# A block-diagonal product in four array tiles of 64 rows by 64 columns, placed between the projections and the transposes, with the projections in the order V, Q, K

## The chip, the cores and the metric

The kernel runs on one core of one Trainium2 chip. The metric is the device time in microseconds of one execution. The kernel before takes 1122.14 us as the median of three runs, from 1119.28 to 1123.42 us.

## The reference, cut to what matters

One transformer block on x of 128 sequences with 32 tokens of 512 features (4096 rows), in fp32. Each sequence has a style id (0 to 15) and an adapter id.

```python
def cond(x, ids, W):                  # W: 16 matrices of 32 x 32
    return einsum('bct,bcd->bdt', x, W[ids])
h = cond(x, itok_B_0_15, cond_weights)
qkv = clip(einsum('bsd,ed->bse', h, w_qkv), -8, 8)
q, k, v = split(qkv); q, k = layer_norm(q), layer_norm(k)
scores = einsum('bqhd,bkhd->bhqk', q, k) * 0.25 + alibi   # 32 heads of 16, causal
x = x + einsum('bsd,ed->bse', softmax(scores) @ v, w_out)
y = einsum('bsi,boi->bso', x, adapter_weight[adapter_ids])
x = x + ffn(y)                        # relu squared, a routed low-rank part, layer norm
```

What matters here is the first line. For each sequence its 32 x 512 slab of x is multiplied, over its 32 token rows, by a 32 x 32 matrix. Tokens mix only inside a sequence.

## The kernel before, in words

**Tiles.** The 4096 rows are cut into 32 tiles of 128 rows, which are four sequences each. The vector engine sorts the sequences by adapter first, so that most tiles have one adapter. The first half of the program handles attention and the adapter product, tile by tile, in a loop over i from 0 to 30 and a tail written out by hand. The second half is the feed-forward part in 8 groups of 4 tiles; the change doesn't touch it.

**The order is written out by hand on every engine.** There is one program per engine, and each iteration of its loop i holds pieces of several tiles at once: the projections of tile i, the transposes of tile i-1, the scores of tile i-2, the softmax-weighted sum of tile i-3, the output projection of tile i-4 and, from i = 6 (`LAG`), the adapter product of tile i-6. Semaphores join the engines: `upto(e, name, t)` makes engine e wait until the step `name` of tile t is done.

**The style product.** GpSimd builds `style_bd`, 128 x 128, which holds the four 32 x 32 matrices of a tile on its diagonal and zeros elsewhere (L1726). TensorE multiplies by it in `style` (L691): four fp32 matmuls, one for each 128 features, with x as the stationary operand and `style_bd` as the moving one; the result, h transposed, fills bank 6. ScalarE rounds it to fp32r as `h_hi` (L1197), VectorE takes the rest as `h_lo` (L1510).

**The projections.** `project` (L701) makes 12 matmuls for each of Q, K and V: high by high, high by low and low by high, over four chunks of features. Q goes to bank 2, K to bank 3, V to bank 5. VectorE clips each out of its bank (`take_q`, `take_k`, `take_v`, L1419), with layer norm statistics for Q and K behind the clip (L1583, L1604).

**One iteration on TensorE, from i = 6.** Projections Q, K, V; `turn_slot` (L796), `turn_values` (L735) and the turns of Q and K (L761), which are transposes in two array tiles of 64 rows by 128 columns; `style` of tile i+1; `scores` (L778) in eight array tiles of 64 rows by 32 columns; `adapt_slot` (L814), 12 matmuls into bank 5; `out_project` (L750), 12 matmuls into bank 6; `values` (L718) in four array tiles of 128 rows by 32 columns. The turned Q and K lie side by side in banks 2 and 3, the turned slot and values in banks 4 and 7.

**The other engines in the same iteration.** VectorE: transpose of the probabilities (L1517), the division (L1465, L1469), clip and statistics of Q, `w_low` (L1424), or `y_low` in the last iterations, clip and statistics of K, clip of V, the low parts `xgT_lo` (L1433), `o_lo` (L1529), `h_lo` (L1510), bias and maximum (L1442, L1446), `q_lo` and the low part of K (L1454, L1460), the residual (L1479). ScalarE: `p_hi` (L1182), a weight chunk, `w_hi` (L1101), normalization of Q and K (L1264), then the high parts `xgT_hi` (L1093), `o_hi` (L1192), `v_hl` (L1256), `h_hi` (L1197), scaling of Q and K (L1227, L1234), their high parts (L1242, L1251), the adapter output `ys` (L1110), the exponential (L1177). GpSimd: two gathers, `w_lo` (L1774), small steps of the layer norm, `p_lo` (L1780), subtraction of the maximum (L1768), the low part of V, `style_bd`.

```python
                for c in range(KC):
                    m = e.matmul(B6[:, P * c:P * c + P], xt[t % XR][:, P * c:P * c + P],
                                 style_bd[t % 2][:, :, :].rearrange("p j d -> p (j d)"), start=True, stop=True)
```

Of the kernel before, what the change touches and what calls it, by code (L numbers as in the profile page):

```python
# [98 lines left out]
def program(nc, x, style_ids, adapter_ids, style_w, wqkv, wo, qk_ln, w2, w_up, w_down, fc1t, expert,  # L99
# [34 lines left out]
    B5, B6 = (psum(f"bank{i}", [P, DM])[:, :] for i in (5, 6))  # L134
# [263 lines left out]
    def values_halved(t):  # L398

        return slot_halved(t + 4 - LAG) and t + 4 >= LAG  # L400

# [16 lines left out]
    with nc.Block() as block:  # L418
# [264 lines left out]
        def _(e):  # L683
            def style(t):

                e.wait_ge(a_x[t % XR], 16 * (t // XR + 1))
                upto(e, "style", t)
                upto(e, "x1", t - 6)
                upto(e, "hlo", t - 1)
                for c in range(KC):  # L690
                    m = e.matmul(B6[:, P * c:P * c + P], xt[t % XR][:, P * c:P * c + P],  # L691
                                 style_bd[t % 2][:, :, :].rearrange("p j d -> p (j d)"), start=True, stop=True)
                m.then_inc(A["h"], 1)
# [108 lines left out]
            def adapt_slot(s, into):  # L802
# [3 lines left out]
                upto(e, "cv" if s < LAST else "cq", s + LAG)  # L806
                if s:
                    e.wait_ge(d_mc, s)
                pairs = [(xgT_hi, w2_lo, c) for c in range(KC)]
# [174 lines left out]
            for i in range(T - 1):  # L984
                if 0 < i < SHORT:
                    style(i + 1)
                project_q(i)
# [5 lines left out]
                project_v(i)  # L993
                if i >= LAG:
                    turn_slot(i - LAG, banks47)
# [7 lines left out]
                if i >= LAG:  # L1003
                    style(i + 1)
# [81 lines left out]
        def _(e):  # L1086
# [107 lines left out]
            def high_h(t):  # L1194
                upto(e, "h", t)
                upto(e, "pv", t - 2)
                e.activation(h_hi[t % 2][:, :, :], B6.rearrange("p (c t) -> p c t", c=KC), ACT.Copy) \  # L1197
# [69 lines left out]
            for i in range(T - 1):  # L1267
# [20 lines left out]
                if i >= LAG:  # L1288
                    slot_in(i - LAG, banks47)
# [3 lines left out]
                if i >= SHORT:  # L1293
                    high_h(i + 1)
# [122 lines left out]
        def _(e):  # L1417
# [89 lines left out]
            def low_h(t):  # L1507
                upto(e, "hhi", t)
                upto(e, "pv", t - 2)
                e.tensor_tensor(h_lo[t % 2][:, :, :], B6.rearrange("p (c t) -> p c t", c=KC),  # L1510
                                h_hi[t % 2][:, :, :].bitcast(F32), ALU.subtract).then_inc(A["hlo"], 1)
# [95 lines left out]
            for i in range(T - 1):  # L1607
                if i >= 3:
                    turn_probs(i - 3)
                if i >= 4:  # L1610
                    divide(i - 4)
                take_q(i)
# [10 lines left out]
                take_v(i)  # L1623
                if i == 0:
                    low_weights(3)
                if i >= LAG:
                    low_slot(i - LAG, banks47)
                if i >= 4:
                    low_o(i - 4)
                if i >= SHORT:  # L1630
# [286 lines left out]
```

## Time and profile before

| | |
|---|---|
| median of three runs | 1122.14 us (1119.28 to 1123.42) |
| profiled execution, its own time | 1117.33 us |
| its span | 1115.5 us |
| mean granted TensorE clock | 0.991 of full |
| TensorE busy | 1068.9 us, 96% |
| VectorE, ScalarE, GpSimd busy | 622.4, 570.1, 565.3 us |

A row of a timeline gives the start in microseconds from the span's start, the length, the engine (PE is TensorE's matmul, PEld its weight load, DVE VectorE, ACT ScalarE, POOL GpSimd), the line of the kernel, the operation, what it writes from what, the array tile for matmuls (rows*columns), the operand shape and how many instructions were merged into the row; in brackets stands idle time before it and who ended it. An fp32 matmul shows as two records, one fp32r or bf16 matmul as one. The length of a matmul record includes its way through the array, so the distance between starts tells the pace.

### The profile page before, as it was taken

Reading aid. Unit: us, or ns where it says so; the run is one execution under the profiler, and the core shown is the slowest. Engines: PE = TensorE matmul, PEld = TensorE weight load, DVE = VectorE, ACT = ScalarE, POOL = GpSimd, SP = SyncE. Lnnn points to the kernel's source line nnn. Section 1 sums busy time; section 2 is a strip of 40 time slices with the busy share of each in tenths; the row PEclk is TensorE's granted clock in tenths of the full one; section 3 lists DMA queues with packets and bytes.
Section 4 is the critical chain, followed back from the end, with each engine's and each line's share of the span. In section 5 each row is a group of like instructions: output and inputs, shape, how many; then the busy total and the mean of one; then the engine's idle time right before and its main releaser. Section 6 shows DMA issues by size and latency. Waiting matters only on the chain.

```text
span 1115.5 us, 28260 instructions
## 1 busy us (share of the span) xinstructions
PE 1068.9 (96%) x11412; PEld 848.4 (76%) x11412; DVE 622.4 (56%) x1050; ACT 570.1 (51%) x955; POOL 565.3 (51%) x490
## 2 busy tenths in 40 slices
PE   5999999999999999999989599999999999999994
PEld 3878888888887888888778476777878787787883
DVE  4677767676766677666765124444544534454432
ACT  3576777777777777777775203424060514232220
POOL 5666877777776767776745112323242323233331
PEclk9999999999999999999999899999999999999998
DMA  6225454555545455555477927443526253130101
GB/s 255 62 79 174 170 185 162 185 167 181 176 171 187 160 187 188 193 159 182 144 263 263 349 89 219 168 95 128 147 71 198 63 192 91 39 85 29 48 29 38
DMA packets 99984, 166.52 MB, mean 149 GB/s; under 512 B 45648, under 2 KB 46416, under 8 KB 96016
## 3 DMA queue, kind: packets, MB, share of 16 engines
q1 hardware_dynamic: 90304, 140.97, 38.5%
q0 software_dynamic: 6064, 17.05, 5.2%
q10 hardware_dynamic: 3488, 6.70, 1.8%
q8 instruction: 92, 1.51, 0.6%
q14 instruction: 36, 0.29, 0.1%
HBM read 98.09 MB, written 40.89 MB: 125 GB/s over the span
## 4 chain that ended last, share of the span: by engine, by line
PE 87%; DMA 3%; issue 3%; POOL 2%; DVE 2%; ACT 1%; SPq 1%; ACTq 0%; DVEq 0%; POOLq 0%
PE pair L934 15%; PE banks L910 15%; PE banks L701 14%; PE bank L750 7%; PE bank L701 7%; PE bank L814 7%; PE bank L927 4%; PE banks L927 4%; PE bank L691 3%; PE pair L718 3%; PE pair L778 2%; PE banks L830 2%; DMA xm<-x_rows 1%; PE banks L880 1%; PE banks L761 1%
## 5 line engine op out<-in xcount | busy, mean ns | idle before, releaser
L1774 POOL TENSOR_TENSOR w_lo<-w2t,w_hi 128x2048 fp32r<-128x2048 f32 x26 | 119.5, 4595 | 70.5 <-ACT w_hi L1101 70.5
L1839 POOL TENSOR_TENSOR u_lo<-act,u_hi 128x512 fp32r<-128x512 f32 x64 | 82.5, 1289 | 124.3 <-ACT u_hi L1313 124.3
L1863 POOL TENSOR_TENSOR frstd<-fve,cst 128x1 f32<-128x1 f32 x32 | 31.9, 996 | 195.9 <-DVE fve L1707 195.9
L1700 DVE TENSOR_TENSOR total<-total,pair 128x512 f32<-128x512 f32 x32 | 22.0, 688 | 168.5 <-PE pair L934 168.5
L701 PE MATMUL banks<-wqkv_hi,h_hi 128*128 128x512 f32 x256 | 103.4, 404 | 0.7 <-DVE wqkv_lo L1575 0.5
L910 PE MATMUL banks<-yT_hi,up_hi 128*128 128x512 f32 x256 | 101.4, 396 | 0.0
L1646 DVE TENSOR_TENSOR act<-act 128x512 f32<-128x512 f32 x59 | 63.0, 1068 | 66.8 <-ACT act L1309 66.8
L701 PE MATMUL banks<-wqkv_hi,h_lo 128*128 128x512 f32 x256 | 99.9, 390 | 0.0
L701 PE MATMUL banks<-wqkv_lo,h_hi 128*128 128x512 f32 x256 | 99.9, 390 | 0.0
L910 PE MATMUL banks<-yT_hi,up_lo 128*128 128x512 f32 x256 | 99.8, 390 | 0.0
L910 PE MATMUL banks<-yT_lo,up_hi 128*128 128x512 f32 x256 | 99.7, 389 | 0.0
L934 PE MATMUL pair<-down_hi,u_hi 128*128 128x512 f32 x256 | 99.6, 389 | 0.0
L934 PE MATMUL pair<-down_lo,u_hi 128*128 128x512 f32 x256 | 99.6, 389 | 0.0
L934 PE MATMUL pair<-down_hi,u_lo 128*128 128x512 f32 x256 | 99.6, 389 | 0.0
L1768 POOL TENSOR_TENSOR probs<-probs,row_max 128x1024 f32<-128x1024 f32 x32 | 61.4, 1918 | 52.4 <-DVE row_max L1446 52.3
L1309 ACT ACTIVATE act<-banks 128x512 f32<-128x512 f32 x64 | 37.9, 592 | 82.6 <-PE banks L910 82.6
L1780 POOL TENSOR_TENSOR p_lo<-probsT,p_hi 128x1024 bf16<-128x1024 f32 x32 | 68.9, 2155 | 9.4 <-ACT p_hi L1182 9.3
L1409 ACT ACTIVATE total<-banks,weight 128x512 f32<-128x512 f32 x16 | 11.0, 687 | 120.5 <-PE banks L927 120.5
L1313 ACT ACTIVATE u_hi<-act 128x512 fp32r<-128x512 f32 x64 | 40.1, 626 | 44.1 <-DVE act L1646 44.0
L910 PEld LDWEIGHTS banks<-yT_hi,up_hi 128*128 128x128 f32 x256 | 48.1, 188 | 13.9 <-issue 4.2
L701 PEld LDWEIGHTS banks<-wqkv_hi,h_hi 128*128 128x128 f32 x256 | 48.0, 188 | 13.2 <-issue 1.4
L701 PEld LDWEIGHTS banks<-wqkv_hi,h_lo 128*128 128x128 f32 x256 | 48.0, 188 | 10.4
(208 smaller groups left out, 2888.6 us busy)
## 6 DMA issues: line engine op xcount, KB each, us to landing
w2t<-in_w SPq DMA_DIRECT2D x26, 1024.0 KB
w<-in_w SPq DMA_DIRECT2D x24, 768.0 KB
vx<-v_hl SPq DMA_DIRECT2D x128, 68.0 KB
x1g<-x_rows SPq DMA_DIRECT2D x32, 256.0 KB, 2.7
kx<-k_hl SPq DMA_DIRECT2D x124, 64.0 KB
x_rows<-x1t SPq DMA_DIRECT2D x31, 256.0 KB, 2.4
y_rows<-ys SPq DMA_DIRECT2D x26, 256.0 KB
w<-in_w SPq DMA_DIRECT2D x24, 256.0 KB, 2.9
```

Source lines behind the costliest of these rows:

```text
L701: m = e.matmul(into, a[:, c, :], b[:, n, c, :], start=(c == 0 and k == 0), stop=(c == KC - 1 and k == 2))
L750: m = e.matmul(B6, a[:, j, :], b[:, j, :], start=(j == 0 and k == 0), stop=(j == BPT - 1 and k == 2))
L814: m = e.matmul(into, a[:, P * c:P * c + P], b[:, c, :], start=(k == 0), stop=(k == len(pairs) - 1))
L910: i = e.matmul((B2, B3)[n % 2], a[:, w, cols], b[m % 2][:, c, :], start=(c == 0 and k == 0), stop=(c == KC - 1 and k == 2))
L927: i = e.matmul((B6, B7)[n % 2], a[m % 2][:, c, toks], b[:, c, :], start=(c == 0 and k == 0), stop=(c == KC - 1 and k == 2))
L934: i = e.matmul(pair[:, n % 2, :], a[f][:, toks], b[:, f, :], start=(f == 0 and k == 0), stop=(f == FC - 1 and k == 2))
L1313: e.activation(u_hi[n % FC][:, :], act[n % 2][:, :], ACT.Copy).then_inc(S["uhi"], 1)
L1646: e.tensor_tensor(act[n % 2][:, :], act[n % 2][:, :], act[n % 2][:, :], ALU.mult) \
L1768: e.tensor_tensor(probs[:, :, :], probs[:, :, :], row_max[:, :].rearrange("p (h o) -> p h o", o=1) .broadcast_to([P, HEADS, SEQ]), ALU.sub ...
L1774: e.tensor_tensor(w2_lo[:, :, :], w2t[:, :, :], w2_hi[:, :, :].bitcast(F32), ALU.subtract).then_inc(d_wlo, 1)
L1780: e.tensor_tensor(p_lo[:, :], probsT[:, :], p_hi[:, :], ALU.subtract).then_inc(A["plo"], 1)
L1839: e.tensor_tensor(u_lo[n % FC][:, :], act[n % 2][:, :], u_hi[n % FC][:, :].bitcast(F32), ALU.subtract) \
```

## The change

From tile 7 on (`style_tiled`), the style product no longer multiplies by the zeros of the block diagonal's off-diagonal halves. Each 128 x 128 x 128 matmul becomes four matmuls with 64 rows, 64 stationary columns and 64 moving columns, each in its own array tile. Row half g writes to bank 5 or 6 by g (`h_at`), so h lies in the first halves of both banks. Since V uses bank 5 too, V is projected and clipped first, and `style` waits for V's clip. `style` moves from behind the turns of K to right behind the K projection, the last of the three now. ScalarE and VectorE make `h_hi` and `h_lo` before the slot's parts instead of behind them. `adapt_slot` writes bank 5 and waits for `h_lo` of the next tile in place of the clip of V.

```diff
-    B5, B6 = (psum(f"bank{i}", [P, DM])[:, :] for i in (5, 6))
+    banks56 = psum("banks56", [P, 2, DM])
+    B5, B6 = banks56[:, 0, :], banks56[:, 1, :]
...
+    def style_tiled(t):
+
+        return t > LAG
+
+    def h_at(t):
+        return half(banks56, 0) if style_tiled(t) else whole(B6)
...
                 upto(e, "hlo", t - 1)
+                if style_tiled(t):
+                    upto(e, "cv", t - 1)
                 for c in range(KC):
-                    m = e.matmul(B6[:, P * c:P * c + P], xt[t % XR][:, P * c:P * c + P],
-                                 style_bd[t % 2][:, :, :].rearrange("p j d -> p (j d)"), start=True, stop=True)
+                    if style_tiled(t):
+                        for k in range(2):
+                            for g in range(ROW_TILES):
+                                rows, at = slice(HALF * g, HALF * g + HALF), HALF * ((g + k) % 2)
+                                m = e.matmul(h_at(t)[at:at + HALF, c, g, :],
+                                             xt[t % XR][rows, P * c + at:P * c + at + HALF],
+                                             style_bd[t % 2][rows, ROW_TILES * g:ROW_TILES * g + ROW_TILES, :]
+                                             .rearrange("p j d -> p (j d)"), start=True, stop=True)
+                    else:
...
-                upto(e, "cv" if s < LAST else "cq", s + LAG)
-                if s:
+                if s == LAST:
+                    upto(e, "cq", s + LAG)
                     e.wait_ge(d_mc, s)
+                else:
+                    upto(e, "hlo", s + LAG + 1)
...
+                if i >= LAG:
+                    project_v(i)
                 project_q(i)
...
                 project_k(i)
                 if i == 0:
                     style(1)
-                project_v(i)
+                if i < LAG:
+                    project_v(i)
                 if i >= LAG:
+                    style(i + 1)
                     turn_slot(i - LAG, banks47)
...
-                if i >= LAG:
-                    style(i + 1)
                 if i >= 2:
                     scores(i - 2)
```

On ScalarE `high_h(i + 1)` stands ahead of `slot_in` from i = 6, on VectorE `take_v(i)` stands ahead of `take_q(i)` and `low_h(i + 1)` ahead of `low_slot`. GpSimd and the DMA queues keep their order.

TensorE, the end of the projections of one iteration in the steady loop, before. The last row of the projections is V's.

```order
L701 MATMUL bank<-wqkv_hi,h_lo 128x512
L796 MATMUL banks<-cst,x1t 128x64 x8
L735 MATMUL banks<-cst,on 128x2x32 x8
L761 MATMUL banks<-cst,qn 128x64 x8
L761 MATMUL banks<-cst,kn 128x64 x8
L691 MATMUL bank<-style_bd,xt 128x128 x4
L778 MATMUL pair<-kx,q_hi 32x128 x8
```

The same place now. The last row of the projections is K's.

```order
L720 MATMUL banks<-wqkv_hi,h_lo 128x512
L705 MATMUL banks<-style_bd,xt 64x64 x16
L815 MATMUL banks<-cst,x1t 128x64 x8
L754 MATMUL banks<-cst,on 128x2x32 x8
L780 MATMUL banks<-cst,qn 128x64 x8
L780 MATMUL banks<-cst,kn 128x64 x8
L797 MATMUL pair<-kx,q_hi 32x128 x8
```

The style product went ahead of the four groups of transposes, and its 4 matmuls became 16 smaller ones.

VectorE in the same iteration, before, from the clip of Q to the bias (`w_low` is the weight chunk):

```order
L1419 TENSOR_SCALAR qn<-banks 128x512
L1583 BN_STATS stats<-qn 128x6
L1424 TENSOR_TENSOR w_low<-banks,w_high 128x512
L1419 TENSOR_SCALAR kn<-banks 128x512
L1583 BN_STATS stats<-kn 128x6
L1604 BN_AGGR mean_var<-stats 128x2 x2
L1419 TENSOR_SCALAR vf<-bank 128x512
L1433 TENSOR_TENSOR xgT_lo<-banks,xgT_hi 128x512
L1529 TENSOR_TENSOR o_lo<-banks,o_hi 128x512
L1510 TENSOR_TENSOR h_lo<-bank,h_hi 128x512
L1442 SCALAR_TENSOR_TENSOR probs<-pair,cst 128x512 x2
```

The same place now:

```order
L1443 TENSOR_SCALAR vf<-banks 128x512
L1443 TENSOR_SCALAR qn<-banks 128x512
L1607 BN_STATS stats<-qn 128x6
L1448 TENSOR_TENSOR w_low<-banks,w_high 128x512
L1443 TENSOR_SCALAR kn<-banks 128x512
L1607 BN_STATS stats<-kn 128x6
L1628 BN_AGGR mean_var<-stats 128x2 x2
L1535 TENSOR_TENSOR h_lo<-banks,h_hi 128x512
L1457 TENSOR_TENSOR xgT_lo<-banks,xgT_hi 128x512
L1553 TENSOR_TENSOR o_lo<-banks,o_hi 128x512
L1466 SCALAR_TENSOR_TENSOR probs<-pair,cst 128x512 x2
```

The clip of V went to the front, and `h_lo` went from third behind the projections' steps to first, right behind the statistics of K.

## Rows read from the trace of the kernel before

**Rows 1.** The page: busy time by engine, and the chain that ended last by engine.

```profile
PE 1068.9 (96%) x11412; PEld 848.4 (76%) x11412; DVE 622.4 (56%) x1050; ACT 570.1 (51%) x955; POOL 565.3 (51%) x490
...
PE 87%; DMA 3%; issue 3%; POOL 2%; DVE 2%; ACT 1%; SPq 1%; ACTq 0%; DVEq 0%; POOLq 0%
```

**Rows 2.** Windows: the steady loop, and one period of it.

```profile
core 0: us, PE busy (x) PEld busy (x) DVE busy (x) ACT busy (x) POOL busy (x), PEclk, DMA share, GB/s
129.00:572.00 443.00, 441.25 (x7072) 360.27 (x7068) 307.05 (x506) 325.41 (x559) 318.57 (x260) 1.00 0.53 178
404.77:423.14 18.37, 18.31 (x296) 14.94 (x293) 12.74 (x21) 13.21 (x24) 13.53 (x11) 1.00 0.55 182
```

**Rows 3.** Timeline of TensorE, one iteration from its first projection to the next one's.

```profile
413.65 0.47 PE L701 MATMUL banks<-wqkv_hi,h_hi 128*128 128x512 f32 x1
...
421.45 0.39 PE L701 MATMUL bank<-wqkv_lo,h_hi 128*128 128x512 f32 x1
421.68 0.39 PE L701 MATMUL bank<-wqkv_hi,h_lo 128*128 128x512 f32 x1
422.00 0.46 PE L796 MATMUL banks<-cst,x1t 64*128 64x64 f32 x8
422.30 0.41 PE L735 MATMUL banks<-cst,on 64*128 64x64 f32 x8
422.55 0.41 PE L761 MATMUL banks<-cst,qn 64*128 64x64 f32 x8
422.80 0.41 PE L761 MATMUL banks<-cst,kn 64*128 64x64 f32 x8
423.14 1.16 PE L691 MATMUL bank<-style_bd,xt 128*128 128x128 f32 x8
424.23 0.25 PE L778 MATMUL pair<-kx,q_hi 64*32 64x128 bf16 x8
424.29 0.24 PE L778 MATMUL pair<-kx,q_lo 64*32 64x128 bf16 x8
424.35 0.29 PE L778 MATMUL pair<-kx,q_hi 64*32 64x128 bf16 x16
...
424.95 0.28 PE L778 MATMUL pair<-kx,q_hi 64*32 64x128 bf16 x8
425.25 0.70 PE L814 MATMUL bank<-w_lo,xgT_hi 128*128 128x512 f32 x2
...
431.97 0.47 PE L701 MATMUL banks<-wqkv_hi,h_hi 128*128 128x512 f32 x1
```

**Rows 4.** Style product over the steady loop: lengths in ns (least/median/most), first and last start.

```profile
L691 PE MATMUL bank<-style_bd,xt x192: 275/275/377, 129.3 to 552.3; 128*128 128x128 f32 x192
```

**Rows 5.** Timeline of PEld: an fp32 product of later, in four array tiles of 32 columns.

```profile
648.35 0.13 PEld L830 LDWEIGHTS banks<-w,xmT 128*32 128x32 f32 x4 [0.30 <-issue]
648.78 0.13 PEld L830 LDWEIGHTS banks<-w,xmT 128*32 128x32 f32 x4 [0.30 <-issue]
```

**Rows 6.** Timeline of TensorE: transposes of full width, in the tail of the loop.

```profile
569.49 0.60 PE L799 MATMUL banks<-cst,x1t 128*128 128x128 f32 x4
569.92 0.60 PE L738 MATMUL banks<-cst,on 128*128 128x128 f32 x4
```

**Rows 7.** Timeline of VectorE, same iteration as rows 3.

```profile
416.67 0.69 DVE L1419 TENSOR_SCALAR qn<-banks 128x512 f32<-128x512 f32 x1 [1.14 <-issue]
...
420.12 0.69 DVE L1583 BATCH_NORM_STATS2 stats<-kn 128x6 f32<-128x512 f32 x1
420.84 0.25 DVE L1604 BATCH_NORM_AGGREGATE mean_var<-stats 128x2 f32<-128x6 f32 x2
422.11 0.69 DVE L1419 TENSOR_SCALAR vf<-bank 128x512 f32<-128x512 f32 x1 [1.01 <-PE bank L701]
...
425.26 0.68 DVE L1510 TENSOR_TENSOR h_lo<-bank,h_hi 128x512 fp32r<-128x512 f32 x1
...
429.39 0.68 DVE L1460 TENSOR_TENSOR k_hl<-banks,k_hl 128x512 bf16<-128x512 f32 x1
...
431.57 1.24 DVE L1517 STREAM_TRANSPOSE probsT<-probs 128x1024 f32<-128x1024 f32 x1
432.73 0.32 DVE L1465 RECIPROCAL recip<-pair 128x32 f32<-128x32 f32 x1
```

**Rows 8.** Timelines of ScalarE and GpSimd, same iteration.

```profile
424.33 0.60 ACT L1197 ACTIVATE h_hi<-bank 128x512 fp32r<-128x512 f32 x1
...
428.52 1.15 ACT L1110 ACTIVATE ys<-bank 128x512 uint16<-128x512 uint16 x2
430.42 1.06 ACT L1177 ACTIVATE probs<-probs 128x1024 f32<-128x1024 f32 x1 [0.75 <-POOL probs L1768]
```

```profile
418.52 4.60 POOL L1774 TENSOR_TENSOR w_lo<-w2t,w_hi 128x2048 fp32r<-128x2048 f32 x1 [1.95 <-ACT w_hi L1101]
```

More of the change, by code:

```diff
@@ L689, in style @@
                 upto(e, "hlo", t - 1)
+                if style_tiled(t):
+                    upto(e, "cv", t - 1)
                 for c in range(KC):
-                    m = e.matmul(B6[:, P * c:P * c + P], xt[t % XR][:, P * c:P * c + P],
-                                 style_bd[t % 2][:, :, :].rearrange("p j d -> p (j d)"), start=True, stop=True)
+                    if style_tiled(t):
[7 more added lines that the diff above has]
+                    else:
+                        m = e.matmul(B6[:, P * c:P * c + P], xt[t % XR][:, P * c:P * c + P],
+                                     style_bd[t % 2][:, :, :].rearrange("p j d -> p (j d)"), start=True, stop=True)
                 m.then_inc(A["h"], 1)
@@ L1196, in high_h @@
                 upto(e, "pv", t - 2)
-                e.activation(h_hi[t % 2][:, :, :], B6.rearrange("p (c t) -> p c t", c=KC), ACT.Copy) \
+                e.activation(h_hi[t % 2][:, :, :].rearrange("p c (g t) -> p c g t", g=ROW_TILES), h_at(t), ACT.Copy) \
                     .then_inc(A["hhi"], 1)
@@ L1288, in _ @@
                 if i >= LAG:
+                    high_h(i + 1)
                     slot_in(i - LAG, banks47)
@@ L1292, in _ @@
                 high_v(i)
-                if i >= SHORT:
+                if SHORT <= i < LAG:
                     high_h(i + 1)
@@ L1509, in low_h @@
                 upto(e, "pv", t - 2)
-                e.tensor_tensor(h_lo[t % 2][:, :, :], B6.rearrange("p (c t) -> p c t", c=KC),
-                                h_hi[t % 2][:, :, :].bitcast(F32), ALU.subtract).then_inc(A["hlo"], 1)
+                hi, lo = (v[t % 2][:, :, :].rearrange("p c (g t) -> p c g t", g=ROW_TILES) for v in (h_hi, h_lo))
+                e.tensor_tensor(lo, h_at(t), hi.bitcast(F32), ALU.subtract).then_inc(A["hlo"], 1)
             def turn_probs(t):
@@ L1611, in _ @@
                     divide(i - 4)
+                if i >= LAG:
+                    take_v(i)
                 take_q(i)
@@ L1622, in _ @@
                 aggregate(i)
-                take_v(i)
+                if i < LAG:
+                    take_v(i)
                 if i == 0:
@@ L1626, in _ @@
                 if i >= LAG:
+                    low_h(i + 1)
                     low_slot(i - LAG, banks47)
@@ L1629, in _ @@
                     low_o(i - 4)
-                if i >= SHORT:
+                if SHORT <= i < LAG:
                     low_h(i + 1)
```

## The prediction

> **What bounds the kernel now.** I read the page first: TensorE is busy for 96% of the span, the other engines for 51 to 56%, and 87% of the chain that ended last is TensorE's [rows 1]. Then the windows: in the steady loop, 443 us long, TensorE has 1.75 us in which it isn't busy, and the granted clock is 1.00, the upper of its two levels [rows 2]. So no other engine holds the loop back. It runs at the pace of what TensorE is given to do, and a cut there shows in full as long as no wait takes its place. Then one iteration in order of time: it starts at 413.65 and the next at 431.97, which is a period of 18.32 us [rows 3]. All estimates are made on this iteration, since the style product shows 192 records from 129.3 to 552.3 (200 are due, 25 tiles by 8; some are missing), and their lengths hardly vary [rows 4].
>
> **What the change touches: 25 tiles.** Tiles 7 to 31 are made in the iterations 6 to 30. Tiles 0 to 6 keep their form.
>
> **Removed: the style product of full width.** It starts at 423.14, and the scores start at 424.23, 1.09 us later [rows 3]. Its eight records are together 1.16 us long, and the last takes 0.275 [rows 4], so the last starts 0.885 us behind the first. The first is 0.10 longer than the others (0.377 against 0.275), since nothing hides its weight load. What is left, 0.785 over seven steps, is a pace of 0.112 us per record. Eight steps and the first load are 0.99 us. The other 0.10 of the 1.09 is the passage to another array shape.
>
> **Such passages don't change in number.** The passage from the transposes of K to the style product costs 0.10 as well: 0.34 from 422.80 to 423.14 where two groups of transposes lie 0.25 apart. From the last projection to the first transposes it is 0.32 where two projections lie 0.23 apart, so 0.09 [rows 3]. Before there were three of them between projections and scores (to 64*128, to 128*128, to 64*32). Now there are three as well (to 64*64, to 64*128, to 64*32).
>
> **Added: 16 matmuls, 32 records, in four array tiles.** No row shows a 64*64 tile, so I bound the pace. A record now moves 64 columns where it moved 128, so alone it would take half of 0.112, that is 0.056 us. If four tiles work side by side, it is 0.014 per record. That they can in fp32 is shown by the product in four tiles of 32 columns: four records start every 0.43 us [rows 5], each with 512 moving columns, for which one alone would need four times 0.112, about 0.45. In the transposes the same is seen in two tiles: four records of full width take 0.43 [rows 6], the same data in eight records of 64 rows 0.25 [rows 3], 0.031 each. The lower bound is the pace of the scores, 8 records in 0.06 to 0.07 us, 0.008 each [rows 3]. The upper bound is 0.056, one tile at a time. I take 0.014, since rows 5 are the nearest: the same kind of number, four tiles, and records of hi and lo parts. 32 by 0.014 is 0.45, plus 0.05 for the first load (the first group of transposes lasts 0.46, the others 0.41 [rows 3]), so 0.50 us against 0.99. **The gain is 0.49 us per tile.**
>
> **The move behind the K projection.** Who waits for the style product, and what now stands behind it? I put the new order on the clock of rows 3, with t the time in that iteration. K's projection ends where V's did, at 421.68 + 0.39 = 422.07. The style product runs from 422.00 to 422.50, the transposes start at 422.59 instead of 422.00, those of Q at 423.14 instead of 422.55, the scores at 423.74 instead of 424.23, the adapter product at 424.76 instead of 425.25.
>
> Three waits become tighter. First, the turn of Q needs K's clip, which frees its bank: the clip now starts where V's did, at 422.11, and ends at 422.80 [rows 7], 0.34 us ahead of 423.14. In the old place K's clip had a whole projection as cover; now 0.34 is left. Second, the adapter product needs `h_lo`. VectorE makes K's clip (to 422.80), the statistics (0.72 by the distance of the starts), their aggregate (0.25) and then `h_lo` (0.68), so it ends at about 424.52 [rows 7]. ScalarE has `h_hi` ready by then: the product ends near 422.65, and 0.60 more [rows 8] is 423.25. So 0.24 us are left to 424.76. This is the smallest margin of the change. Third, the next V projection, at the head of the next iteration, now needs the adapter output out of bank 5. ScalarE starts that at 428.52 and ends at 429.67 [rows 8], and the next iteration starts at 431.48 instead of 431.97, with 1.8 us to spare. The low part of K, needed there too, ends at 430.07 [rows 7].
>
> **What costs nothing, and its cover.** The clip of V is only moved. The first of the three clips waited for its projection before and does so now. The slot's high part on ScalarE is made about 0.6 later, at 423.4 instead of 422.83, since it needs the transposes that moved back; its end at 424.0 is covered by the scores, up to 424.76. The scaling of Q behind the four high parts keeps its place within 0.1, as the same four stand ahead of it. The low part of the adapter weights on GpSimd ends at 418.52 + 4.60 = 423.12 [rows 8]; the shorter period makes it at most 0.49 later in an iteration, 423.6, still ahead of 424.76. The exponential ends at 430.42 + 1.06 = 431.48 [rows 8], and VectorE's transpose behind it is pinned to that, so it moves from 0.40 ahead of the next iteration to its very start; with the division behind it (1.1 us) it is done 2.3 us into the iteration, and the first clip is due 3.02 us into it (416.67 less 413.65 [rows 3, 7]). The DMA queues keep their order, and their mean share is 0.53 to 0.55 [rows 2].
>
> **The sum.** 25 tiles by 0.49 us are 12.2 us. The profiled execution took 1117.33 us (span 1115.5 and 1.8 around it), so it would take 1105.1. The runs shown lie higher, with the median at 1122.14, and against that the forecast is 1109.9, say **1110 us**, 1.1% less. A measurement of this kernel tells about 0.5%, 5.6 us, from no change.
>
> **Rivals.**
>
> *The pace per record doesn't fall with tiles of this form.* Small fp32 records of 64 columns may cost a fixed amount each. The nearest row is the transposes', 0.031 each. Then 32 records take 1.0 us and, with the first load, 1.04 against 0.99: 25 times 0.05 is 1.3 us more, **1123 us**, no change. Hi and lo records that follow each other in the same tile would give about the same: 16 matmuls of two by 0.056, half hidden, are 0.9. For it: the only 64-row fp32 rows in the trace show this pace. Against it: those use two tiles, where two by 0.014 is what two-way overlap would show anyway, and the scores go at 0.008 with 128 columns. Chance 0.15. The Trainium skill (TensorE: Matmul & The Clock Gate, Back-to-back issue gap) has a rule of this kind: between 1 and 64 columns a matmul costs about 60 cycles, some 25 ns. By its figure the product would take an estimated 0.85 us and the kernel about 1119. The trace disagrees for bf16 [rows 3], where 8 ns are seen; for fp32 in 64*64 tiles no row shows it.
>
> *The wait for `h_lo` takes half of the gain.* If VectorE ends it 0.5 us later than I put it (a semaphore on each of four steps, a slower read over two banks), the adapter product stands for 0.26 us in each iteration. The gain is 0.23 by 25, 5.8 us: **1116 us**. For it: the margin of 0.24 is two or three hand-overs long. Against it: the four durations are all in the rows. Chance 0.12.
>
> *Slower: one tile at a time.* If loads in two column halves of the same rows, or the hi and lo records, keep the four tiles from overlapping, each record takes its 0.056. Then the product is 32 by 0.056 and 0.05, 1.84 us against 0.99. That is 0.85 by 25, 21 us more: **1143 us**. It decides from a pace of 0.036 per record, where the kernel is over 0.5% slower (0.99 + 0.22 = 1.21 us). Against it: rows 5 show four column tiles overlapping on the same rows, and rows 3 show row tiles doing so. Chance 0.07.
>
> **How the numbers follow.** The forecast has the rest, 0.66. All of it is faster by over 0.5%, and of the second rival about half; 0.72 in all. Slower by over 0.5% are the last rival and a little for a wait that I don't see: 0.09. Within 0.5% is what is left, 0.19. The range: at the lower bound of the pace, 0.008, the product takes 0.31, the gain is 0.68 by 25, 17 us, so 1105. Upwards it takes in the second rival and stops at 1122, just short of the first. About 0.2 is left out.
>
> **What would show each step.** The new style rows should be 32 records within 0.45 us from first start to last, and the period 17.8 us instead of 18.32. The distance from the last projection to the first score should be 2.06 us instead of 2.55. In the waits of TensorE no `h_lo` and no K clip should appear; `h_lo` should end before the adapter product starts. I'm wrong if the style records stand 0.03 or more apart, or if the gap between scores and adapter product grows beyond the 0.30 that now lie between the last score row and it [rows 3].

## The result, and the profile after

The changed kernel takes 1130.19 us in the median of four runs (1129.04 to 1139.29), the kernel before 1122.34 (1119.28 to 1123.42, four runs). The ratio is 1.0096 with an interval of 1.0069 to 1.0123: slower by 1.0%, where 1.1% faster was forecast. The profiled execution took 1129.4 us. That of the kernel before took 1117.33 us, 5.0 less than its median, so a difference of the two traces (12.1 us by the spans) overstates that of the medians, which is 7.9 us.

The page of the changed kernel: span, busy time by engine, and the chain that ended last by engine.

```profile
span 1127.6 us, 29460 instructions
...
PE 1064.7 (94%) x12012; PEld 843.4 (75%) x12012; DVE 643.6 (57%) x1050; ACT 574.0 (51%) x955; POOL 567.8 (50%) x490
...
PE 81%; DVE 6%; issue 3%; DMA 3%; POOL 3%; ACT 1%; SPq 1%; ACTq 0%; DVEq 0%; POOLq 0%
```

Against [rows 1], TensorE has 4.2 us less to do, and yet the span is 12.1 us longer. VectorE is busy for 21.2 us more with the same 1050 instructions, and its share of the chain went from 2% to 6%. So some of VectorE's instructions became longer, and TensorE waits for them.

Windows of the changed kernel split the loop in two; the last row is the first iteration of its late stretch. The columns are those of [rows 2].

```profile
125.00:430.00 305.00, 300.53 (x5360) 244.64 (x5359) 216.73 (x356) 223.04 (x388) 228.75 (x187) 1.00 0.53 178
430.00:585.00 155.00, 141.41 (x2354) 114.64 (x2353) 114.62 (x158) 108.04 (x175) 94.00 (x75) 0.96 0.53 163
427.00:446.00 19.00, 15.88 (x297) 12.93 (x282) 15.64 (x21) 13.98 (x23) 11.39 (x11) 0.91 0.52 146
```

Up to 430 the loop is as in [rows 2]: TensorE has 4.5 us in 305 in which it isn't busy, and the granted clock is 1.00. Behind 430 it isn't busy for 13.6 us in 155, and the granted clock is 0.96 on the mean: part of that stretch runs at 1.2 GHz in place of 2.4 (from 442.60 to 445.00 the granted clock is 0.50). The waits of TensorE in each of the two stretches, of the changed kernel (us in total, times, longest):

```profile
PE pair L797 <- issue: 2.5, 2, 1.6
```

```profile
PE banks L780 <- DVE kn L1443: 13.0, 7, 3.0
```

All of the late idle time is one wait, made seven times: the turn of Q waits for K's clip.

**The steady iteration** did what was forecast. Timeline of TensorE, changed kernel, the iteration before the late stretch, the counterpart of [rows 3].

```profile
418.07 0.39 PE L720 MATMUL banks<-wqkv_hi,h_lo 128*128 128x512 f32 x1
418.39 0.69 PE L705 MATMUL banks<-style_bd,xt 64*64 64x64 f32 x32
419.01 0.46 PE L815 MATMUL banks<-cst,x1t 64*128 64x64 f32 x8
...
420.15 0.25 PE L797 MATMUL pair<-kx,q_hi 64*32 64x128 bf16 x8
...
421.13 1.16 PE L835 MATMUL banks<-w_lo,xgT_hi 128*128 128x512 f32 x4
...
426.76 0.22 PE L737 MATMUL pair<-vx,p_hi 128*32 128x68 bf16 x4
...
427.97 0.47 PE L720 MATMUL banks<-wqkv_hi,h_hi 128*128 128x512 f32 x1
```

The 32 style records start at 418.39 and the next group at 419.01. The distance from the last projection to the first score is 2.08 us (2.06 was forecast, 2.55 it was), and the adapter product starts 0.98 behind the first score, as before. The iteration started at 410.01, so the period is 17.96 us against 18.32. K's clip ends at 419.19 here (it starts at 418.50), 0.37 us ahead of the turn of Q at 419.56; 0.34 was forecast.

**A late iteration**, the next one. The same view:

```profile
436.33 0.69 PE L705 MATMUL banks<-style_bd,xt 64*64 64x64 f32 x32
...
440.68 0.46 PE L780 MATMUL banks<-cst,qn 64*128 64x64 f32 x8 [3.02 <-DVE kn L1443]
...
442.60 2.07 PE L835 MATMUL banks<-w_lo,xgT_hi 128*128 128x512 f32 x4
```

The style product is as quick as ever. The turn of Q stands for 3.02 us, and behind it the same four records of the adapter product last 2.07 us instead of 1.16. Why K's clip is late shows in the timelines of VectorE and of GpSimd, same iteration.

```profile
433.72 0.69 DVE L1443 TENSOR_SCALAR qn<-banks 128x512 f32<-128x512 f32 x1 [2.03 <-PE banks L720]
...
435.05 0.68 DVE L1448 TENSOR_TENSOR w_low<-banks,w_high 128x512 fp32r<-128x512 f32 x1
435.64 4.38 DVE L1509 TENSOR_TENSOR y_low<-y_word,y_high 128x512 fp32r<-128x512 f32 x1
439.95 0.68 DVE L1443 TENSOR_SCALAR kn<-banks 128x512 f32<-128x512 f32 x1
```

```profile
434.93 4.55 POOL L1802 TENSOR_TENSOR w_lo<-w2t,w_hi 128x2048 fp32r<-128x2048 f32 x1 [4.13 <-ACT w_hi L1124]
```

`y_low`, the low part of an output plane, is made in the iterations from 24 on, where `low_planes` stands between the clips of Q and K. In iteration 24 it comes behind `w_low`; in the six behind it the weight chunks are done, and it stands in `w_low`'s place. It is 4.38 us long and ends at 440.02. GpSimd's `w_lo` runs from 434.93 to 439.48. The kernel before has both in this iteration too; these rows of it were not among those read for the prediction. VectorE, then GpSimd, kernel before:

```profile
436.92 0.68 DVE L1485 TENSOR_TENSOR y_low<-y_word,y_high 128x512 fp32r<-128x512 f32 x1
437.71 0.69 DVE L1419 TENSOR_SCALAR kn<-banks 128x512 f32<-128x512 f32 x1
```

```profile
438.58 4.57 POOL L1774 TENSOR_TENSOR w_lo<-w2t,w_hi 128x2048 fp32r<-128x2048 f32 x1 [3.80 <-ACT w_hi L1101]
```

There `y_low` takes 0.68 us and is done 0.98 us before `w_lo` starts (0.5 to 0.6 us in the six iterations behind it). Counted from the start of the iteration, `w_lo` starts 6.6 us in before and 7.0 now, while `y_low` went from 4.95 to 7.67: it stands behind Q's clip, and that moved back by one projection when V went to the front. It fell from ahead of `w_lo` into it. In all seven it ends 0.54 to 0.56 us behind the end of `w_lo`, whenever it started: nearly its whole 0.68 us is still to be done when `w_lo` ends. The kernel before shows the same thing once, beside another instruction of GpSimd that was not among the rows read either. The eighth `y_low`, in the tail behind the loop, takes 1.98 us and ends 0.55 behind `p_lo`:

```profile
573.87 1.98 DVE L1485 TENSOR_TENSOR y_low<-y_word,y_high 128x512 fp32r<-128x512 f32 x1
```

```profile
573.14 2.16 POOL L1780 TENSOR_TENSOR p_lo<-probsT,p_hi 128x1024 bf16<-128x1024 f32 x1
```

The chain that ended last of the changed kernel, from 433 to 446, goes just that way (start, us, what):

```profile
435.73 4.30 DVE y_low L1509
440.03 0.61 DVE kn L1443
...
440.68 0.72 PE banks L780 x16
```

**The account.** Iteration 24 starts at 427.97 now and at 431.97 before: by then 4.0 us are gained. Its last seven periods are 22.6, 21.1, 19.8, 21.3, 19.8, 21.3 and 19.8 us, together 145.7, against 129.3 before (18.3 each and 19.3 in the last, where the adapter product stands 1.13 us for issue), 16.4 more. From -4.0 and +16.4 come +12.4 at the end of the loop, and +12.1 in the span. In four of the seven (22.6, 21.1, 21.3 and 21.3 us) the granted clock is 0.92; beyond the steady period and their wait they are 1.5 to 1.6 us longer, 6.2 together. In the three of 19.8 it is 1.00, and they are 0.2 to 0.3 longer. The waits don't tell the two kinds apart: 3.02, 1.61, 1.78 and 1.85 us in the four, 1.54, 1.55 and 1.64 in the three.

### The profile page after: what moved, and what is told of

Read it like the earlier page. It is cut to its first block, busy times and chain, and to the rows that moved or that the text cites. A ratio compares the mean times of both kernels' runs of the same rounds, so it can differ in the third digit from the quotient of the medians.

```text
span 1127.6 us, 29460 instructions
## 1 busy us (share of the span) xinstructions
PE 1064.7 (94%) x12012; PEld 843.4 (75%) x12012; DVE 643.6 (57%) x1050; ACT 574.0 (51%) x955; POOL 567.8 (50%) x490
## 4 chain that ended last, share of the span: by engine, by line
PE 81%; DVE 6%; issue 3%; DMA 3%; POOL 3%; ACT 1%; SPq 1%; ACTq 0%; DVEq 0%; POOLq 0%
PE banks L720 18%; PE pair L955 15%; PE banks L931 14%; PE banks L948 8%; PE banks L769 7%; PE banks L835 6%; PE pair L737 2%; DVE y_low L1509 2%; PE pair L797 2%; PE banks L851 2%; DMA xm<-x_rows 2%; PE banks L901 1%; PE banks L780 1%; PE banks L705 1%; POOL probs L1796 1%
## 5 line engine op out<-in xcount | busy, mean ns | idle before, releaser
L720 PE MATMUL banks<-wqkv_hi,h_hi 128*128 128x512 f32 x384 | 153.4, 399 | 3.1 <-DVE wqkv_lo L1599 0.5
L720 PE MATMUL banks<-wqkv_hi,h_lo 128*128 128x512 f32 x384 | 149.8, 390 | 0.0
L720 PE MATMUL banks<-wqkv_lo,h_hi 128*128 128x512 f32 x384 | 149.7, 390 | 0.0
L1433 ACT ACTIVATE total<-banks,weight 128x512 f32<-128x512 f32 x32 | 22.0, 687 | 186.2 <-PE banks L948 186.2
L720 PEld LDWEIGHTS banks<-wqkv_hi,h_hi 128*128 128x128 f32 x384 | 72.0, 188 | 20.7 <-issue 6.1
L720 PEld LDWEIGHTS banks<-wqkv_hi,h_lo 128*128 128x128 f32 x384 | 72.1, 188 | 15.5
L720 PEld LDWEIGHTS banks<-wqkv_lo,h_hi 128*128 128x128 f32 x384 | 72.2, 188 | 14.5 <-issue 0.5
```

The source lines that it names most:

```text
L720: m = e.matmul(into, a[:, c, :], b[:, n, c, :], start=(c == 0 and k == 0), stop=(c == KC - 1 and k == 2))
```

## The experiments

My theory: VectorE's `y_low` stands still for as long as GpSimd's `w_lo` runs beside it, and the change is slower only for this meeting. The tiles and the order V, Q, K are a gain. The rivals: the order or the late h makes the stall by itself; `y_low` is only slow by its two sources or its layout; the tiles give nothing. Every ratio is against the kernel before on the same chip.

**The planes ahead of Q's clip.** The changed kernel, `low_planes` moved ahead of the place that slipped:

```diff
                 if i >= LAG:
                     take_v(i)
+                if i >= T - 8:
+                    low_planes(i - T + 8)
                 take_q(i)
...
-                if i >= T - 8:
-                    low_planes(i - T + 8)
                 take_k(i)
```

> The changed kernel with y_low moved on VectorE from behind the clip of Q to between the clips of V and Q. Exclusion theory (y_low reads two SBUF tensors and stands still while GpSimd makes w_lo): here it runs from about 5.1 us into the iteration, before w_lo starts (7.0 us), so its eight records take 0.68 us each, TensorE's wait for the clip of K is gone in the last seven iterations, their period is 17.95 us as in the others, the granted clock stays at the upper level, and the kernel takes 1111 to 1114 us. Rival (y_low is late because its input or its store is late, or VectorE is slowed whatever stands next to it): the records stay at 2 to 4 us and the time at 1125 to 1132 us.

Measured: 1114.46 us against 1121.9, ratio 0.9938 (0.9917 to 0.9959). One execution in ten took 5916 us, which no profile explains; it is left out of the ratio. The time is 0.5 us above the upper end of what was expected. All eight `y_low` (least/median/most in ns), the late stretch, and TensorE's waits for issue from 125 to 600:

```profile
L1509 DVE TENSOR_TENSOR y_low<-y_word,y_high x8: 685/692/2269, 434.2 to 570.7; 128x512 fp32r<-128x512 f32 x8
```

```profile
430.00:585.00 155.00, 148.56 (x2634) 120.50 (x2635) 109.50 (x178) 119.32 (x199) 102.86 (x82) 1.00 0.61 187
```

```profile
PE pair L797 <- issue: 6.1, 4, 1.8
```

Moving one instruction of VectorE turns 1.0% slower into 0.6% faster. Seven of the eight `y_low` are back at 0.69 us; the one of 2.27 is the eighth, beside `p_lo` as in the kernel before. The wait for K's clip is gone, and the granted clock of the late stretch is back at 1.00, so the slower clock was a result of the waits. The period is 17.95. Something new shows as well: four stalls of TensorE in the scores, in which it waited for nothing that the profile names. In the scores of the kernel before there is none; its loop has one of 1.13 us, in the adapter product at 554.62.

**The same meeting in the kernel before.** The kernel before, with nothing of the change, and `low_planes` moved back behind the statistics of K:

```diff
                 if 0 <= i - 5 < CHUNKS:
                     low_chunk(i - 5)
-                if i >= T - 8:
-                    low_planes(i - T + 8)
                 take_k(i)
                 stats_of(i, 1, kn, "ck")
                 aggregate(i)
+                if i >= T - 8:
+                    low_planes(i - T + 8)
```

> The kernel before, untiled, with y_low moved behind the statistics of K, so that it starts while GpSimd makes w_lo. Exclusion theory: the records grow from 0.68 to some 3.5 us though nothing of the change is in the program. What stands behind it (clip of V, then the low parts) comes 3 us late, but the clip of K is ahead of it, so TensorE loses at most 1 us in each of seven iterations: 1122 to 1130 us. Rival (the longer records are brought about by the new banks, tiles or order): the records stay at 0.68 us and the time at 1122 us.

Measured: 1128.09 us, ratio 1.0056 (1.0031 to 1.0080). VectorE and GpSimd in that kernel, and a wait of TensorE:

```profile
443.22 4.38 DVE L1485 TENSOR_TENSOR y_low<-y_word,y_high 128x512 fp32r<-128x512 f32 x1
447.53 0.68 DVE L1419 TENSOR_SCALAR vf<-bank 128x512 f32<-128x512 f32 x1
```

```profile
442.49 4.58 POOL L1774 TENSOR_TENSOR w_lo<-w2t,w_hi 128x2048 fp32r<-128x2048 f32 x1 [3.79 <-ACT w_hi L1101]
```

```profile
PE bank L814 <- DVE vf L1419: 7.0, 7, 1.3
```

The stall comes without tiles and without the new order: 4.38 us again, to the hundredth. Here it makes the clip of V late, by which the adapter product waits 1.0 us in each of the seven iterations, whose periods are 19.0 to 19.5. It costs less than in the changed kernel, since more of TensorE's work stands between the stalled step and the one that needs it. That the order or the late h makes the stall falls with this run. The trace shows a second thing: TensorE's waits from 125 to 435, in this kernel without a single style tile, have two stalls for issue in the scores, at 206.36 and 410.68.

```profile
PE pair L778 <- issue: 3.0, 2, 1.5
```

**GpSimd waits for the plane.** The changed kernel, the collision taken away on the other side:

```diff
+                if i >= T - 8:
+                    e.wait_ge(p_low, i - T + 9)
                 if i >= LAG:
                     low_w2(i - LAG)
```

> The changed kernel with one wait more: in the last eight iterations GpSimd starts w_lo only behind y_low. Exclusion theory: y_low is back at 0.68 us, the clip of K is not late, but w_lo ends some 1.4 us later, at 13 us into the iteration, and the adapter product waits for it 1 to 1.5 us in seven iterations: 1118 to 1123 us. Rival (y_low long by itself): its records stay at 2 to 4 us and the time gets worse than 1130 us, since w_lo now comes behind them.

Measured: 1130.32 us, ratio 1.0076 (1.0053 to 1.0098). All `y_low`, then two of TensorE's waits from 420 to 600:

```profile
L1509 DVE TENSOR_TENSOR y_low<-y_word,y_high x8: 673/676/681, 435.6 to 581.1; 128x512 fp32r<-128x512 f32 x8
```

```profile
PE banks L835 <- POOL w_lo L1802: 9.7, 6, 1.9
PE banks L835 <- issue: 6.9, 1, 6.9
```

The length of `y_low` follows the theory: 0.68 us, all eight. The time doesn't: no gain was had, since `w_lo` now starts behind `y_low`, and the adapter product needs it. Its margin in [rows 8] was that of an iteration without planes. The two steps have to stand one behind the other in either order, and only with `y_low` first and early, as in the first experiment, did neither wait show up. The stall of 6.9 us is named issue, but the trace explains it: the added wait holds for the last tile too, whose plane, the eighth, is made late in the tail (581.13 to 581.81). `w_lo` starts only behind it, and the adapter product at 586.65, 0.2 us behind its end.

```profile
581.95 4.50 POOL L1802 TENSOR_TENSOR w_lo<-w2t,w_hi 128x2048 fp32r<-128x2048 f32 x1 [13.66 <-DVE y_low L1509]
```

So 6.9 us of this run's time are the edit's own, and its total (1118 to 1123 us was expected) says little of what the other seven iterations would cost.

**What about `y_low` makes it stand still?** Three runs, on the changed kernel each. With one source, and the subtraction left out:

```diff
-                e.tensor_tensor(y_low[:, :], y_word[:, :], y_high[:, :].bitcast(F32), ALU.subtract).then_inc(p_low, 1)
+                e.tensor_scalar(y_low[:, :], y_word[:, :], 2.0 ** -12, None, ALU.mult).then_inc(p_low, 1)
```

> The changed kernel with y_low made from y_word alone times a constant, in the same place; it leaves out the subtraction of the high part for the first two groups of the feed-forward part. If two source tensors are what excludes GpSimd, the records are some 0.7 us long and the kernel takes 1111 to 1114 us. If any fp32 operation of VectorE from SBUF to SBUF in its fast form is excluded, they stay at 2 to 4 us and the time at 1130 us.

With both sources, every second word:

```diff
+                lo, word, hi = (v.rearrange("p (t n) -> p n t", n=2)
+                                for v in (y_low[:, :], y_word[:, :], y_high[:, :].bitcast(F32)))
+                e.tensor_tensor(lo, word, hi, ALU.subtract).then_inc(p_low, 1)
```

> The changed kernel with y_low in its late place and of the same two sources, but reading and writing every second word (an access pattern of two rows of 256 words with a step of 2). If it is the fast form of an fp32 operation between SBUF tensors that GpSimd excludes, this slower form runs beside w_lo and takes some 0.7 to 1.2 us, the clip of K is at most 0.5 us late, and the kernel takes 1113 to 1118 us. If any operation with two SBUF sources is excluded, the records stay at 2 to 4.4 us and the time at 1130 us.

With one source and every second word, the subtraction left out again:

```diff
+                lo, word = (v.rearrange("p (t n) -> p n t", n=2) for v in (y_low[:, :], y_word[:, :]))
+                e.tensor_scalar(lo, word, 2.0 ** -12, None, ALU.mult).then_inc(p_low, 1)
```

> The changed kernel with y_low in its late place, made from y_word alone times a constant (as e4) and with every second word read and written (as e7); it leaves out the subtraction of the high part in the first two groups of the feed-forward part. If an operation is excluded beside w_lo when it has two SBUF sources or a fast form, this one has neither, its records are some 0.7 to 1.2 us long and the kernel takes 1113 to 1118 us. If every elementwise fp32 operation from SBUF to SBUF is excluded, they stay at 2 to 4.4 us and the time at 1130 us.

One execution each: 1131.31, 1130.79 and 1126.7 us. All `y_low` of the first, of the second, and VectorE in a late iteration of the third, where `w_lo` runs from 434.86 for 4.55 us:

```profile
L1509 DVE TENSOR_SCALAR y_low<-y_word x8: 1812/3446/4155, 437.2 to 589.0; 128x512 fp32r<-128x512 f32 x8
```

```profile
L1511 DVE TENSOR_TENSOR y_low<-y_word,y_high x8: 2079/3608/4315, 435.7 to 587.4; 128x512 fp32r<-128x512 f32 x8
```

```profile
435.00 0.68 DVE L1448 TENSOR_TENSOR w_low<-banks,w_high 128x512 fp32r<-128x512 f32 x1
435.59 4.11 DVE L1510 TENSOR_SCALAR y_low<-y_word 128x512 fp32r<-128x512 f32 x1
```

All three stand still, to 4.2 and 4.3 us at most and 4.11 in the row, so a second source isn't needed, and the layout doesn't matter. But the third was meant to have no fast form, and the trace speaks against that: with one source `y_low` ends 0.28 to 0.30 us behind `w_lo` in the plain layout and with every second word alike, and with two sources 0.53 to 0.57. Twice as fast in either layout, it may well have had the fast form in both. That one source is held only in a fast form is therefore not ruled out by these runs. What isn't slowed beside `w_lo`: `w_low` in the same rows, one source of which is a bank (0.68 us at 435.00), and the statistics of K in the steady iteration (0.69 at 420.12, inside `w_lo` from 418.52 to 423.12 [rows 7, 8]). All that stood still here read and write SBUF alone, element by element; one SBUF source alone, as in the statistics, isn't enough to be held.

**The tiles alone.** The mended kernel of the first experiment, with the style product of full width and the rest of the change kept:

```diff
     def style_tiled(t):
 
-        return t > LAG
+        return False
```

> As e1 (y_low between the clips of V and Q), but with the style product of full width in every tile: the new order and banks without the tiles. If the tiles give 0.37 us per tile and the order nothing, the period is 18.35 to 18.45 us, and the kernel takes 1122 to 1125 us, no faster than the kernel before. If the order gives a part, the period is under 18.3.

Measured: 1124.53 us, ratio 1.0033 (1.0015 to 1.0050). Timeline of TensorE:

```profile
406.94 0.39 PE L720 MATMUL banks<-wqkv_hi,h_lo 128*128 128x512 f32 x1
407.17 1.05 PE L710 MATMUL banks<-style_bd,xt 128*128 128x128 f32 x8
408.15 0.46 PE L815 MATMUL banks<-cst,x1t 64*128 64x64 f32 x8
...
409.29 0.25 PE L797 MATMUL pair<-kx,q_hi 64*32 64x128 bf16 x8
```

The period is 18.21 us; 18.35 to 18.45 was expected, so this missed. Behind K's projection the untiled product saves a passage: it starts 0.23 behind the last projection, which is the pace of the projections. So of the 0.37 that the whole change takes off the period, the tiles give 18.21 - 17.95 = 0.26, and the order and the place alone 0.12. In the style product itself, from its first record to the slot's, it is 0.98 against 0.62. 25 tiles by 0.26 are 6.5 us. The ratios are 0.0095 apart, 10.7 us, so some 4 us of the difference between these two kernels are not in the steady periods. In the profiles they can be placed. The spans are 9.9 us apart (1122.2 and 1112.3); 24 periods by 0.26 are 6.2. Another 1.1 lies ahead of iteration 7, where only the untiled kernel has a stall for issue (1.49 us in the scores at 113.90). The rest, 2.6, is in single iterations: two of the untiled kernel take 22.0 and 21.6 us, with stalls for issue of 2.1 and 2.0 and a granted clock of 0.92, where the longest of the other takes 19.9.

**One wait fewer.** In the changed kernel the distance from the values to the next projection grew from 1.11 to 1.20 us. With V first, six waits of TensorE stand ahead of the first projection, where five did. One of them is met from the second tile on:

```diff
             def project(t, n, into, name):
                 upto(e, "hlo", t)
-                e.wait_ge(s_wlo, n + 1)
+                if t == 0:
+                    e.wait_ge(s_wlo, n + 1)
```

> As e1, but TensorE waits for the low parts of the weights only in tile 0 and no longer ahead of each of the 93 later projections, where that wait is long satisfied. The projection at the head of an iteration now has six waits and starts 1.21 us behind the first values record where it was 1.11 with five. If the number of waits in front of it is what costs 0.10, the distance goes back to about 1.11 to 1.15, the period to 17.85, and the kernel gains 2 to 3 us on e1 (1111 to 1113). If it is something else, the period stays at 17.95 and the time at 1114.

The edit drops this wait ahead of all three projections of an iteration. Measured, on top of the first experiment's edit: **1112.06 us**, ratio 0.9921 (0.9902 to 0.9940). Timeline of TensorE:

```profile
390.14 0.22 PE L738 MATMUL pair<-vx,p_hi 128*32 128x68 bf16 x4
...
391.23 0.47 PE L721 MATMUL banks<-wqkv_hi,h_hi 128*128 128x512 f32 x1
```

The distance is 1.09 us, and the period 17.84: a wait that was met long ago cost 0.11 us per iteration, all of it at the head, where TensorE changes from the values to the projections. This kernel is faster than both. Against the first experiment's the totals alone don't separate it, since the intervals overlap; the period does.

**The stalls in the scores.** Their place in TensorE's instruction stream was moved by satisfied waits at its head, 96 and then 192 of them:

```diff
             e.wait_ge(A["ones"], 1)
+            for _ in range(96):
+                e.wait_ge(A["ones"], 1)
```

> As e6, with 96 waits that are satisfied at the head of TensorE's program, where it idles 8 us anyway; nothing else differs but where in the instruction stream each block lies. The stalls of 1 to 2.4 us that the waits list puts down to issue come at the scores of iterations 9 and 18 in every tiled kernel, and in none of the kernel before. If they depend on where a refill of the instruction buffer falls, they move to other iterations or go away, and the time is 1107 to 1113 us. If they belong to something in those iterations (a DMA, a bank), they stay at the scores of iterations 9 and 18.

> As e9 with 192 waits. Same theories: the stalls move by another step or go away (1107 to 1113 us), or they stay where they are in e6.

Measured: 1112.77 us, ratio 0.9914 (0.9880 to 0.9947), with 96, and 1116.32, ratio 0.9940 (0.9918 to 0.9963), with 192. The second is above the 1107 to 1113 us that were expected. Rows of TensorE's timeline with such a stall: of the changed kernel, then with 96 waits, then with 192.

```profile
167.71 0.24 PE L797 MATMUL pair<-kx,q_hi 64*32 64x128 bf16 x5 [0.89 <-issue]
...
331.25 0.24 PE L797 MATMUL pair<-kx,q_hi 64*32 64x128 bf16 x4 [1.59 <-issue]
```

```profile
133.29 0.24 PE L798 MATMUL pair<-kx,q_lo 64*32 64x128 bf16 x6 [1.03 <-issue]
...
295.32 0.21 PE L798 MATMUL pair<-kx,q_lo 64*32 64x128 bf16 x1 [0.99 <-issue]
...
458.68 0.23 PE L798 MATMUL pair<-kx,q_hi 64*32 64x128 bf16 x3 [1.82 <-issue]
```

```profile
225.50 0.25 PE L798 MATMUL pair<-kx,q_hi 64*32 64x128 bf16 x7 [1.76 <-issue]
...
388.30 0.23 PE L798 MATMUL pair<-kx,q_hi 64*32 64x128 bf16 x1 [1.99 <-issue]
```

In these three kernels the stall comes back after 162 to 164 us, nine iterations or some 2,850 matmul records, and it moves when instructions are put ahead. So it goes by the place in TensorE's own stream, and not by data, a semaphore or a time. It isn't brought by the tiles: the two kernels with the style product of full width have it too, at 206.36 and 410.68 (the kernel before with the late plane) and at 207.27 and 411.57 (the one with tiles taken out), 204 us or eleven iterations apart, which are some 3,220 records. So the distance is no fixed number of matmuls. Moving it doesn't remove it: the total is 5.3 us in three stalls without added waits (with one more of 1.2 in the adapter product), 4.1 in four with 96, and 6.5 in four with 192, of which two (at 425.59 and 572.07) lie outside the series. That it is the fetching of instructions would fit; no record shows the fetch, and what sets the distance stays open.

## Why the prediction was wrong

**The step that failed** is the cover of K's clip. The prediction gave it 0.34 us ahead of the turn of Q, on VectorE's rows of one iteration, and said that no clip of K would show in TensorE's waits. In the steady iteration that held (0.37). In seven iterations the turn of Q waits for it, 1.9 us on the mean, up to 3.0. Two choices led there. First, "All estimates are made on this iteration": the style rows hardly vary over the loop, and so I took the iteration at 413.65 for all 25. They say nothing of VectorE, which makes `y_low` in the last seven (on top of `w_low` in the first of them, in its place in the other six), exactly between the clips of Q and K, and the cover of K's clip was the thinnest margin but one. Second, I placed steps of VectorE by the lengths that they had in the kernel before. `y_low` had 0.5 to 1.0 us to spare against `w_lo`, which no view of waits shows, because nothing waits there. That such a meeting makes it longer stood in the trace of the kernel before, in the eighth `y_low` (1.98 us beside `p_lo`). The prediction moved Q's clip by a projection, 2.7 us, and never asked what is queued behind it and beside what it would then run.

**The rivals.** The slower one, one tile at a time, is not what happened: the mechanism was none of the three. The range ended at 1122, and the time came out at 1130.19. A wait that wasn't seen had a place in the prediction, but only 0.02 of the chances (0.09 less the 0.07 of the slower rival), and neither a mechanism nor a price.

**What was right.** The pace: the distance to the slot's transposes is 0.62 us for 32 records, 0.60 was implied (0.50 and a passage of 0.10). From first to last start they take 0.48 (the group's 0.69 less the last one's own 0.2), 15 ns each, where 14 were taken. That four 64*64 tiles in fp32 work side by side is settled, and both rivals on the pace fall. By the some 25 ns per matmul of the Trainium skill (TensorE: Matmul & The Clock Gate, Back-to-back issue gap) these 32 records would take an estimated 0.8 us if each counts as a matmul, and the trace shows 0.48. Counted as the 16 matmuls that they are, the estimate is 0.4, and this row doesn't speak against the page; the 8 ns of the scores, one record per bf16 matmul [rows 3], do, for matmuls in different tiles. The wait for `h_lo`, the rival with a chance of 0.12, didn't come: adapter product 0.98 behind the first score, as before. The low part of K, the adapter output and the exponential were covered as said.

**What was off in size.** The period: 17.95 where 17.83 was forecast. 0.10 to 0.11 of the 0.12 is the sixth wait ahead of V's projection, which was not costed; taking it out gives 17.84. And the stalls in the scores, not foreseen: 2.5 us up to iteration 24. Without the collision the kernel comes out in the range but short of the forecast: 25 by 0.37 is 9.3 us where 12.2 were forecast, and by the medians the first experiment is 7.4 us faster than before; with the wait out as well it is 9.7, at 1112.06. By the spans of the two traces it is only 3.2 (1112.3 against 1115.5), since the first experiment's has 6.1 us of stalls in the scores, and that of before is of an execution 5 us below its median.

**The mechanism of the loss**, by the runs. Shown: `y_low` is 0.68 us with GpSimd's long instructions out of its way and up to 4.38 beside `w_lo`, in both kernels; with `y_low` early the change is 0.6% faster. The Trainium skill (SBUF — State Buffer, Who interferes with whom) says that VectorE and GpSimd share one pair of SBUF ports, which whoever issues first has for its whole instruction. By that section a VectorE instruction contends when it has two SBUF inputs and GpSimd reads SBUF, or when it runs in a 2-port mode, which `tensor_scalar` can; with at most one SBUF input outside these modes it doesn't. The traces agree: `y_low` with two sources and with one is held to the end of `w_lo`, and `w_low` (one bank, one SBUF source) and the statistics (one SBUF source) keep their 0.68 and 0.69 us. Whether the one-source `y_low` ran in such a mode no record says; its end 0.29 us behind `w_lo` instead of 0.55 fits it. 13.0 of the 16.4 us are the waits themselves. Some 6 us more come from the granted clock (by the windows, 155 by 0.04; by the four periods, 6.2), 0.8 from the three other late periods, and against them go the gain of the steady period, seven by 0.37 or 2.6, and the stall of some 1.0 us that the kernel before has in its last iteration.

## What to carry to other kernels

When a change moves a step of an engine by some microseconds, follow everything that is queued behind it, in every kind of iteration (the first, the steady and the last ones), and lay its new place against what the other engines do at that time, VectorE's against GpSimd's long instructions above all. A length in a profile is the length beside those neighbours, and a record of the same step that is longer than the rest (here 1.98 us against 0.68) names the neighbour to keep away from; a margin that costs nothing shows in no view of waits. And where TensorE is the bound, a wait that has long been met, ahead of its first product, still has a price.

## What the runs showed of the hardware that I had not expected

- An elementwise fp32 instruction of VectorE from SBUF to SBUF, 128x512, takes 0.68 us, and up to 4.38 beside a GpSimd instruction of 4.55 that it can't pass; with one source and every second word it is still 4.11. It ends 0.55 us behind that instruction with two sources, 0.29 with one. One that reads a bank, and the statistics, keep their 0.68 and 0.69.
- Four fp32 tiles of 64 by 64 start 32 records of 64 columns in 0.48 us, 15 ns each, while the same product of full width took 0.112 us per record of 128 columns.
- A satisfied wait more ahead of TensorE's next product, behind a product of another array shape, takes 0.11 us per iteration (1.20 to 1.09).
- TensorE stands for 0.9 to 2.4 us with nothing waited for, mostly in the scores: every 162 to 164 us with the tiles, every 204 us in the two untiled kernels that show it.
- After waits of 3.02, 1.61, 1.78 and 1.85 us in four of seven iterations the granted clock was 0.92 over the iteration, and 1.5 to 1.6 us were lost beside the wait; after 1.54, 1.55 and 1.64 us in the other three it stayed at 1.00. Behind stalls for issue of 2.1 and 2.0 us it was 0.92 as well, behind one of 2.35 it stayed at 1.00.
